# Four groups of weighted sums a tile in place of two, in the cross-attention of a decoder layer

## The reference, cut to what matters

```
qk  = einsum('bdm,bdn->bmn', qh, kh) * scale     # qh, kh, vh: (512, 8, 256)
sm  = softmax(qk, axis=-1)
ret = einsum('bmn,bcn->bcm', sm, vh)
```

## Time and profile before

| | |
|---|---|
| median of 3 runs | 1825.08 us (1822.34 to 1825.66) |
| the profiled execution | 1829.2 us, span 1827.2 us |
| mean granted TensorE clock | 0.983 of full speed |
| busy over the span: PE, PEld | 94%, 76% |
| busy over the span: DVE, ACT, POOL | 65%, 45%, 46% |
| maxima, L1195 | 256, 308.9 us |
| exponentials, L1143 | 512, 292.0 us |
| turned scores, L1295 | 1024 matmuls, 229.5 us |
| scores, L1284 | 1024 matmuls, 171.4 us |
| weighted sums, L1310 | 2048 matmuls, 125.5 us |

### The profile page before, as it was taken

The page is one execution under the profiler, slowest core; times in us unless marked ns, Lnnn a source line. Parts: engine busy times, 40 slices in busy tenths (PEclk is TensorE's granted clock), DMA queues, the critical chain, the costliest instruction groups (busy, mean ns, idle before and its releaser), DMA issues. The chain is left out here.

```text
span 1827.2 us, 45302 instructions
## 1 busy us (share of the span) xinstructions
PE 1724.7 (94%) x15345; PEld 1385.0 (76%) x15441; DVE 1184.1 (65%) x2269; ACT 816.4 (45%) x1579; POOL 838.5 (46%) x1302
## 2 busy tenths in 40 slices
PE   3999999999999999999869999999999899999997
PEld 2788888888888888888757777777776899766664
DVE  5777777777777777777668788788886454322221
ACT  3434334334334334334317777777777534211111
POOL 4455555555555555554443444444444331144443
PEclk9999999999999999999879999999999999999999
DMA  5021121121121121121233444444443366322221
GB/s 186 19 59 41 47 57 41 45 57 43 43 57 43 43 57 43 43 57 39 61 90 100 121 122 124 119 121 120 119 119 93 97 187 229 105 65 66 69 63 36
DMA packets 145343, 148.43 MB, mean 81 GB/s; under 512 B 26194, under 2 KB 139926, under 8 KB 143482
## 3 DMA queue, kind: packets, MB, share of 16 engines
q1 hardware_dynamic: 138362, 120.87, 24.3%
q0 software_dynamic: 5760, 14.06, 2.4%
q10 hardware_dynamic: 1152, 12.58, 2.2%
HBM read 93.46 MB, written 54.11 MB: 81 GB/s over the span
## 5 line engine op out<-in xcount | busy, mean ns | idle before, releaser
L1195 DVE TENSOR_REDUCE xmax<-bankX 128x4 f32<-128x1024 f32 x256 | 308.9, 1217 | 63.7 <-PE bankX L1284 58.8
L1143 ACT ACTIVATE xe<-bankXT 128x512 f32<-128x512 f32 x512 | 292.0, 598 | 93.6 <-PE bankXT L1295 79.4
L1295 PE MATMUL bankXT<-stq,stk 98*128 98x256 f32 x1024 | 229.5, 310 | 11.9 <-ACT xe L1143 5.4
L369 POOL TENSOR_TENSOR roped<-ropeC,ropeD 128x512 f32<-128x512 f32 x160 | 205.1, 1289 | 57.0 <-DVE ropeD L530 57.0
L1295 PEld LDWEIGHTS bankXT<-stq,stk 98*128 98x128 f32 x1024 | 156.0, 191 | 55.3 <-ACT xe L1143 36.1
L557 DVE TENSOR_TENSOR oTl<-bankV,oTh 128x512 fp32r<-128x512 f32 x128 | 88.2, 689 | 166.8 <-ACT oTh L445 166.8
L662 PE MATMUL bankQ<-wqh,xnTh 128*128 128x512 f32 x384 | 188.9, 492 | 0.0
L1284 PE MATMUL bankX<-stk,stq 96*128 96x256 f32 x1024 | 171.4, 292 | 14.8 <-DMA rw<-in_rw 10.9
L361 POOL TENSOR_TENSOR prob<-prob,rden 128x1024 f32<-128x1024 f32 x64 | 121.9, 1904 | 88.9 <-DVE rden L553 88.9
L1284 PEld LDWEIGHTS bankX<-stk,stq 96*128 96x128 f32 x1024 | 145.1, 196 | 18.8 <-DMA rw<-in_rw 11.1
L1800 PE MATMUL bankX<-wexp,xT 128*128 x320 | 152.1, 599 | 2.3 <-DVE xT L1666 2.3
(11 more groups left out here) (189 smaller groups left out, 3884.9 us busy)
## 6 DMA issues: line engine op xcount, KB each, us to landing
stackk_d<-chl SPq DMA_DIRECT2D x96, 128.0 KB, 2.3
stackq_d<-q2hl SPq DMA_DIRECT2D x96, 128.0 KB, 2.3
stk<-stackk_d SPq DMA_DIRECT2D x32, 384.0 KB
stq<-stackq_d SPq DMA_DIRECT2D x128, 96.0 KB
wexp<-in_wexp ACTq DMA_DIRECT2D x8, 1536.0 KB, 8.3
x_d<-x SPq DMA_DIRECT2D x64, 128.0 KB, 1.9
xrden<-inv_d SPq DMA_DIRECT2D x64, 128.0 KB, 2.5
xin<-xg_d SPq DMA_DIRECT2D x40, 128.5 KB, 2.1
```

The costliest lines, as they stand in the source:

```text
L369: nc.gpsimd.tensor_tensor(roped[c % 3][:], ropeC[c % 2][:], ropeD[c % 2][:], ALU.add).then_inc(s_rsum, 1)
L1143: nc.scalar.activation(xe[q][:].rearrange("p n m -> p (n m)"), bT[:, q % 2, :], ACT.Exp).then_inc(s_xe, 1)
L1195: nc.vector.tensor_reduce(xmax[tile[1] % 2][:, :, a:b + 1:b - a].rearrange("p m h -> p h m"), bS[:, 2 * (pr % 2):2 * (pr % 2) + 2, :].rear ...
L1295: ins = nc.tensor.matmul(bT[:, q % 2, n * D:(n + 1) * D], stk[p][0:98, hd // 4, n * P:(n + 1) * P], stq[p][0:98, hd, :], start=True, stop= ...
```

## The change

The weighted sums of a tile are computed in four groups of 16 matmuls (four heads each), behind steps 0, 2, 4 and 6, in place of two groups of 32 behind steps 1 and 5. The semaphore `s_xp` counts four a tile, and its waits follow. The exponentials of a tile ask four times for room in `xe`, not twice. `evac_sums` moves from step 6 to step 7 on ScalarE, and `invert` from behind the maximum of step 0 to behind that of step 1 on VectorE. SP's and POOL's orders are not edited.

```
# ScalarE
-                need(act, s_xp, (at(w) - 1) * 2)
+                need(act, s_xp, (at(w) - 1) * 4)
...
-                act.wait_ge(s_xp, (at(v) + 1) * 2)
+                act.wait_ge(s_xp, (at(v) + 1) * 4)
...
-                if q % 8 == 0:
-                    need(act, s_xp, at(w) * 2 + q // 8 - 1)
+                if q % 4 == 0:
+                    need(act, s_xp, at(w) * 4 + q // 4 - 3)
...
-                    if three and r == 6:
+                    if three and r == 7:
                         evac_sums(v)
# VectorE
                     if one:
                         max_x(tile, r)
-                    if four and r == 0:
+                    if four and r == 1:
                         invert(z)
# TensorE
-            def results_x(v, g):
+            def results_x(v, b):
...
-                pe.wait_ge(s_xe, at(v) * XH + 8 * g + 8)
-                if g == 0:
+                pe.wait_ge(s_xe, at(v) * XH + 4 * b + 4)
+                if b == 0:
                     pe.wait_ge(s_cT, at(v) + 1)
                     need(pe, s_nd, at(v))
-                for b in (2 * g, 2 * g + 1):
-                    for k in range(2):
-                        for j in range(4):
...
+                for k in range(2):
+                    for j in range(4):
...
-                    if three and r == 1:
-                        results_x(v, 0)
-                    if three and r == 5:
-                        results_x(v, 1)
+                    if three and r % 2 == 0:
+                        results_x(v, r // 2)
```

More of the change, by code:

```diff
@@ L1297, in turned_scores_x @@
                 ins.then_inc(s_xst, 1)
-            def results_x(v, g):
+            def results_x(v, b):
                 c = cT[v[1] % 2][:].rearrange("p k h c -> p k (h c)")
-                pe.wait_ge(s_xe, at(v) * XH + 8 * g + 8)
-                if g == 0:
+                pe.wait_ge(s_xe, at(v) * XH + 4 * b + 4)
+                if b == 0:
                     pe.wait_ge(s_cT, at(v) + 1)
                     need(pe, s_nd, at(v))
-                for b in (2 * g, 2 * g + 1):
-                    for k in range(2):
-                        for j in range(4):
[L1309 to L1314, removed]
+                for k in range(2):
+                    for j in range(4):
+                        m = (j + b) % 4
+                        ins = nc.tensor.matmul(bN[32 * j:32 * j + 32, 0, (m % 2) * D:(m % 2 + 1) * D],
+                                               c[:, k, 160 * j + 32 * m:160 * j + 32 * m + 32],
+                                               xe[4 * b + j][:, k, :],
+                                               start=(b == 0 and k == 0), stop=(b >= 2 and k == 1),
+                                               skip_group_check=True)
                 ins.then_inc(s_xp, 1)
```

## The result

The changed kernel takes 1911.86 us (median of 4 runs, 1899.06 to 1913.57), against 1825.37 us for the kernel before, timed beside it. The ratio is 1.0461, with a 95% interval of 1.0425 to 1.0497: 86.5 us slower. The forecast was 1876, with a range up to 1904. Its sign held; the time lies 8 us outside its range.

The account below looks back on a forecast made before the run. It took cross-attention to be bound by TensorE, busy 97.71 of 100 us. To the profiled 1829.2 us it added 42 for longer tiles and 9 for the clock: 1880, or 1876 against the median; range 1856 to 1904.

Parts of the forecast that it names:

- The mechanism: Cross-attention: later `invert` delays SP's `sh` copies, holding the turned scores that open step 4: 8.87 us after step 0's, against 7.15.
- T0 to T8: From the turned scores opening step 4 to those opening the next step 0: 7.41 us, against 7.52 before.
- The undisturbed tile: One cross-attention tile without a clock fall: 16.28 us, 1.46 more than before, 42 us over 29 tiles.
- The cover of the reciprocals: Between POOL's product and sum and the statistics that read them: 3.4 us, which the longer tile keeps.
- The splitting: Four groups of weighted sums for two: each extra group costs 0.34 us for changing tiling, 0.68 a tile.
- The smoothing: A group behind each even step removes most TensorE waits for exponentials: 1.28 less 0.41, a gain of 0.87 us a tile.
- T8's wait: The turned scores opening step 0 still wait for their exponential, behind the `nd` copy and row scaling: 0.41 us.
- rival 1: No change: `sh` copies never late, a tile of 14.73 us against 14.82, -3 us, 1822; chance 0.05.
- The sign by the table of waits: In the waits table, weight loads' waits for exponentials would go down to about one a tile.
- the clock term: Clock falls at the new TensorE pause: one tile in four, 7 x 1.3 = 9 us; bounds 0 and 43 us.
- Rival 3: The clock falls in nearly every tile at the new TensorE pause: 1910 us; chance 0.07.
- rival 2: Faster: the array changes tiling at no cost and the copies are in time, 22 us off, 1803; chance 0.05.

Follow-up runs that it names:

- experiment 3: Changed kernel with SP issuing the two `sh` copies ahead of the two copies of the reciprocals: 1938.46 us, ratio 1.0600 to the kernel before.
- experiment 1: Changed kernel with `invert` back behind the maximum of step 0, four groups and later `nd` copy kept: 1825.08 us, ratio 0.9989 to the kernel before.
- experiment 4: Changed kernel with 12 extra matmuls of 256 columns ahead of TensorE's wait for `sh`: 1875.10 us, ratio 1.0273 to the kernel before.
- experiment 2: Kernel before with only `invert` moved, to behind the maximum of step 1: 1887.42 us, ratio 1.0310.
- experiment 8: As experiment 1, but with two groups of 32 behind steps 2 and 6 in place of four: 1883.74 us, ratio 1.0301 to the kernel before.
- experiment 7: Kernel before with its second group of 32 split into two of 16, one change of tiling more a tile: 1833.89 us, ratio 1.0044.
- experiment 6: Kernel of experiment 2 with 7 extra matmuls of 256 columns ahead of TensorE's wait for `sh`: 1855.84 us, ratio 1.0164 to the kernel before.
- experiment 10: Experiment 1 with row scaling in step 6, POOL's weight before its quotient, and SP's next-tile loads first: 1905.98 us, ratio 1.0397 to the kernel before.
- experiment 5: Changed kernel with six extra matmuls of 256 columns, not twelve, ahead of TensorE's wait for `sh`: 1884.51 us, ratio 1.0307 to the kernel before.

## Why the prediction was right, and where it was wrong

**The mechanism** was right. The chain from the second maximum over the reciprocal and SP's order to `sh` and T0 stands in the rows link by link: from T8 (1214.22) to S(1) 2.77 us, 0.79 to the maximum, 1.14 to the reciprocal, 0.37 to SP, 1.34 to the `sh` copies, 2.92 to T0 (1223.55): 9.33 in place of 8.87. Only the first link is off, by 0.40, and only in this tile and four others of the 27 between 993 and 1476 us. In the other 22 it is 2.37 to 2.39, as forecast, and T8 to T0 is 8.94 in the median. The five are those in which S(0) was held. Its load at 1214.85 puts 0.33 us down to the maximum, but the one that it needs began at 1211.81 and took 1.23 us. The last piece of the tile's loads landed at 1214.72 by the trace: in this tile S(0) waited for them. The forecast had left such holds out, though the kernel before has them too: its S(0) mostly loads 0.23 us behind T8, but in one tile 0.97. T0 to T8 took 7.39 (1206.83 to 1214.22), forecast 7.41. The undisturbed tile was forecast at 16.28 us and measured at 16.38; the pause at 42 us, and measured at 45 by the intervals and at 48.5 by filling it.

The cover of the reciprocals was read wrong, without a cost here: the 3.4 us of the earlier trace rows are those of the statistics, but in experiment 3 the weight behind the quotient on POOL was the first to be late.

**The splitting** was right: 0.25 to 0.31 us a group, forecast 0.34. **The smoothing** fits: T8's wait, forecast at 0.41 (its terms add up to 1.64, not 1.69, so 0.36), shows 0.46, and experiment 1 puts splitting and smoothing together at 0 to 4 us faster; the forecast of TensorE's own order (14.73 against 14.82, rival 1's 3 us) is inside that. No run prices the smoothing by itself. The sign by the table of waits failed: waits "for exponentials" did not go down to one a tile, since up to three of the idle times behind groups carry that label.

**The step that failed** is the clock term: "I take one tile in four: 7 x 1.3 = 9 us." The clock fell in 16 of the 29 tiles. Ten falls cost 1.3 to 1.5 us each, as in the bound; six lasted three times as long and cost 4.6 us each. Together they are 41 us by the intervals and 38 by experiment 4. Two things were wrong in the term. The chance of a fall, one tile in four, has no reason in the text. It was set between two pauses of the third stage, which stand behind matmuls of 256 columns, where this one stands behind four matmuls of 8 columns. The prediction named them, even with 2.2 us with hardly a column, as long as the pause that brought a fall, and kept to the low chance. Experiments 2 and 8 show falls behind 1.30 and 0.84 us, under the 1.39 that brought none there. And the bound for a fall took the low stretch of 3.4 us for the only kind. The trace of the kernel before had a longer one, at the end of cross-attention, from 1411.8 us for 6.8 us:

```profile
1412.00:1413.00 1.00, 0.56 (x2) 0.26 (x2) 0.00 (x0) 1.00 (x4) 0.93 (x2) 0.50 0.16 46
...
1417.00:1418.00 1.00, 1.00 (x13) 0.19 (x5) 0.00 (x0) 0.00 (x0) 0.00 (x0) 0.50 0.80 262
```

No weight load had waited for more than 0.66 us in the 7 us before it. With both numbers right, the sum would have been 1825 + 42 + 41 = 1908, inside the runs' 1899 to 1914. Rival 3 comes near that time (1910) by luck: it had a fall in nearly every tile and none of them long, where 16 falls, six of them long, came to about the same sum.

**Rivals 1 and 2** needed the `sh` copies in time; 27 waits at T0 refute both, and experiment 7 refutes the free change-over again. Rival 1's world is the one of experiment 1: no change.

## What to carry to other kernels

Before a producer is moved by one step, follow every in-order queue that waits for it, and list what is queued behind the wait: here two `sh` copies, which need nothing of the reciprocals, stood behind them on SP, with 0.2 us to spare. A new pause of TensorE has two prices, its length and the clock, and where little work stands before it, the second can be as large as the first; if the pause can't be avoided, matmuls that only fill it bring that part back (experiments 4 and 6). And several slacks in such a loop hang together: three of the moves tried here (experiments 3, 8 and 10) took one wait or cost away, opened another, and ended 57 to 112 us above the kernel before.

## What the runs showed of the hardware

**A stretch at the low clock has no single length.** After some pauses the granted clock was at 0.50 for 3.4 us, after others for 10 us (1223.4 to 1233.6) and 13 us (1197 to 1210, experiment 2), with PE busy all through the rows shown of both. At 1.2 GHz each step takes longer, but what else separates the long falls from the short isn't settled here.

**Pauses well under 1.4 us can bring it down, and their length alone doesn't decide**: 0.84 us in experiment 8 and 1.30 us in experiment 2 were followed by 0.50, while 1.39 us in the earlier trace rows were not. Of pauses of about 1 us, 12 of 15 were followed by a fall in experiment 2, directly behind matmuls of 8 columns, and 1 of 24 in experiment 5, behind six of 256.

**The idle time at a change of tiling doubles at the low clock.** Behind a group of strips the next full load waits 0.41 us at full clock; at 1.2 GHz it is 0.81, and inside the group sets of four wait too, 0.22 us:

```profile
1225.55 0.20 PEld L1309 LDWEIGHTS bankN<-xe,cT 128*32 128x32 f32 x8 [0.22 <-issue]
...
1227.42 0.50 PEld L1295 LDWEIGHTS bankXT<-stq,stk 98*128 98x128 f32 x2 [0.81 <-issue]
```

A group then takes 1.87 us (1225.55 to 1227.42), against 1.00.
